# A fused retention and mixture-of-experts kernel on one core: the last shared-down tiles move behind the output product, and steps 7 to 9 are reordered

## What is computed

```
q, k, v, g = x@w + b            (8 heads of 32; q and k rotated)
sim   = (q k^T / sqrt(32)) * decay mask (causal)
ret   = group_norm(sim @ v) * gn_weight + gn_bias
x1    = layernorm(x + (silu(g) * ret) @ w_o + b_o)
shared = (silu(x1@shared_gate) * (x1@shared_up)) @ shared_down
routed = top-1 of 8 experts, score s = sigmoid(logit):
         (up * silu(gate)) @ down_proj, gate|up = (s*x1)@gate_up_proj
out   = layernorm(x1 + shared + routed)
```

## Time and profile before

| | us |
|---|---|
| median of three runs (lowest, highest) | 561.33 (559.33, 561.43) |
| the profiled execution, its own time | 561.59 |
| its span in the trace | 559.8 |
| TensorE busy | 538.6 (96%) |
| VectorE, ScalarE, GpSimd busy | 410.0, 229.4, 338.3 |
| SyncE | only starts transfers |
| mean granted clock of TensorE, share of full | 0.988 |

### The profile page before, as it was taken

How to read it: one execution, slowest core, us unless ns; L and a number is a source line. 1 busy time by engine, 2 the same in 40 slices (tenths; PEclk the granted TensorE clock), 3 DMA queues, 4 the chain that set the end, 5 groups by cost and what they waited for, 6 DMA issues and landing times.

```text
span 559.8 us, 11796 instructions
## 1 busy us (share of the span) xinstructions
PE 538.6 (96%) x3830; PEld 454.4 (81%) x3830; DVE 410.0 (73%) x892; ACT 229.4 (41%) x410; POOL 338.3 (60%) x330
## 2 busy tenths in 40 slices
PE   8999989999999999999997889999999999999994
PEld 6777778788788788788886678888888888888884
DVE  5896986887887887887974678757866666666664
ACT  4435532454553552552542765133333333333331
POOL 1956695475475575774683385716786556566644
PEclk9999999999999999999998899999999999999998
DMA  8920507605405306304296823765677666666651
GB/s 264 318 93 3 187 1 49 217 0 98 168 1 162 104 2 138 128 0 151 77 358 171 305 109 114 255 198 181 198 184 211 192 183 179 183 198 194 196 181 38
DMA packets 46554, 83.82 MB, mean 150 GB/s; under 512 B 11360, under 2 KB 30576, under 8 KB 46480
## 3 DMA queue, kind: packets, MB, share of 16 engines
q1 hardware_dynamic: 38720, 64.52, 37.4%
q0 software_dynamic: 6112, 15.40, 10.2%
q10 hardware_dynamic: 1664, 3.15, 1.6%
HBM read 61.11 MB, written 22.34 MB: 149 GB/s over the span
## 4 chain that ended last, share of the span: by engine, by line
PE 81%; POOL 5%; issue 5%; DVE 4%; DMA 4%; SPq 1%; ACT 1%; POOLq 0%; DVEq 0%; ACTq 0%
PE duo L1731 42%; PE duo L2190 9%; PE duo L2021 5%; PE duo L1811 4%; DMA dn_raw<-L_ffn_down_proj 4%; PE duo L1836 3%; PE duo L2200 3%; PE duo L1893 3%; PE duo L2025 2%; POOL rstd L1014 2%; PE duo L2011 1%; PE duo L2076 1%; PE duo L2003 1%; PE duo L1925 1%; POOL turned L977 1%
## 5 line engine op out<-in xcount | busy, mean ns | idle before, releaser
L1731 PE MATMUL duo<-w_gu_hi,xsT 128*128 x320 | 107.2, 397 | 0.0
L1731 PE MATMUL duo<-x1T,wsgu 128*128 128x512 f32 x384 | 91.1, 393 | 1.5 <-DVE x1T L1237 1.5
L1731 PEld LDWEIGHTS duo<-x1T,wsgu 128*128 128x128 f32 x384 | 71.4, 188 | 17.1 <-DVE x1T L1237 2.5
L1147 POOL DMA_INDIRECT out_rows<-of,seat x39 | 39.5, 1012 | 56.7 <-DVE of L1688 55.0
L1731 PEld LDWEIGHTS duo<-w_gu_hi,xsT 128*128 128x128 f32 x320 | 59.7, 188 | 11.2
L1731 PE MATMUL duo<-w_gu,xsT 128*128 x160 | 62.0, 388 | 0.0
L1643 DVE SCALAR_TENSOR_TENSOR eh<-duo,seat,e_act 128x512 f32<-128x512 f32 x38 | 28.5, 751 | 39.9 <-PE duo L1731 39.9
L1220 DVE TENSOR_TENSOR sims<-duo,causal 128x512 f32<-128x512 f32 x64 | 41.1, 684 | 21.0 <-ACT sims L719 20.4
L977 POOL TENSOR_TENSOR turned<-turned,swapped 128x1024 f32<-128x1024 f32 x16 | 38.5, 2405 | 29.7 <-DVE swapped L1211 29.7
L1138 POOL DMA_INDIRECT xz<-xz_d,seat x39 | 45.8, 1173 | 8.9 <-issue 8.8
L1077 POOL DMA_INDIRECT seat_d<-stage,place_i x32 | 35.7, 1117 | 18.9 <-DVE place_i L1479 9.6
(11 more groups left out here) (214 smaller groups left out, 1292.0 us busy)
## 6 DMA issues: line engine op xcount, KB each, us to landing
dn_rest<-dn_lo_d SPq DMA_DIRECT2D x39, 512.0 KB, 4.5
w_gu<-L_ffn_gate_up_proj SPq DMA_DIRECT2D x8, 1024.0 KB, 9.7
x_in<-x_t SPq DMA_DIRECT2D x8, 512.0 KB, 6.9
x_res<-L_attn_x SPq DMA_DIRECT2D x8, 512.0 KB, 4.0
dn_raw<-L_ffn_down_proj SPq DMA_DIRECT2D x8, 512.0 KB, 9.6
dn_hi_d<-dn_top SPq DMA_DIRECT2D x8, 512.0 KB, 7.5
dn_lo_d<-dn_low SPq DMA_DIRECT2D x8, 512.0 KB, 8.5
xz_d<-zs SPq DMA_DIRECT2D x8, 512.0 KB
```

The costliest lines, as they stand in the source:

```text
L1147: pool.indirect_dma_start(out, bass.IndirectOffsetOnAxis(ap=seat[:, s, 1:2], axis=0), of[:, s % OUTS, :], None).then_inc(sig.out_done[s % ...
L1731: last = mm(out_, left(a, k), right(b, k), start=start and k == 0 and n == 0, stop=stop and k == kt - 1 and n == len(PASSES) - 1)
```

## The change

Three things change.

1. **Deferral.** In steps 3 to 7 (`DEFERRED`) TensorE no longer takes `shared_down(f, 1)` ahead of `output(a)`. It takes it in the next step, between the second quad of `similarities` and the first of `values`. VectorE's `shared_sum(f, 1)` and SyncE's `sums_out` move with it into the next step (steps 4 to 8).
2. **Steps 7 to 9.** `PARTED` gives step 4 two experts (3 and 4) and step 7 one (7). In step 8 TensorE takes the second half of the last `gate_project`, behind `ret_transposes`; ScalarE, VectorE and the loads follow that (experts 1 and 3 change places, the load of expert 1 waits longer, the load of expert 0 starts earlier). `first_norm` of pair 6 is done in two parts, `statistics` and `moments` of it stand earlier on VectorE. The first product of step 9 takes its passes so that it needs the high half of `x1T` first.
3. **Group norm and step 2.** `group_rstd` works on each half as soon as its variance is there, in all steps. In step 2 `swap(2, 1)`, `turn(2, 1)`, `residual(1)` and `x_lo(3)` are taken later.

The core of the diff (line numbers are those of before):

```diff
 HALF_FF = FF // 2
-PARTED = {1: (0,), 2: (1,), 3: (2,), 4: (3,), 5: (4,), 6: (5,), 7: (6, 7)}
+PARTED = {1: (0,), 2: (1,), 3: (2,), 4: (3, 4), 5: (5,), 6: (6,), 7: (7,)}
+DEFERRED = range(3, PAIRS)
 SEATS = (EXPERTS - 1) * TOKENS + SLOTS * P
...
                     down_raw_in(PARTED[t][0])
+                if t - 1 in DEFERRED:
+                    sums_out(t - 3)
                 if has(t - 2):
...
                 if t == PAIRS - 1:
-                    sp.wait_ge(sig.g_ps, KT * PAIRS)
+                    sp.wait_ge(sig.qk_ps, 4 * PAIRS)
                     gate_up_in(0)
-                    gate_up_in(1)
                     sp.wait_ge(sig.turned_ok, 2 * PAIRS)
...
                 if t == PAIRS:
-                    sp.wait_ge(sig.o_ps, 2 * (PAIRS - 1))
-                    gate_up_in(7)
                     sp.wait_ge(sig.s_ps, 8 * PAIRS)
                     gate_up_in(2)
+                    sp.wait_ge(sig.o_ps, 2 * (PAIRS - 1))
+                    sp.wait_ge(sig.g_ps, KT * PAIRS)
+                    gate_up_in(1)
+                    gate_up_in(7)
                 if t == PAIRS + 1:
...
                     down_raw_in(PARTED[t][1])
-                if has(t - 2) and t < PAIRS:
+                if has(t - 2) and t < PAIRS and t not in DEFERRED:
                     sums_out(t - 2)
...
                     act.wait_ge(sig.g_ps, KT * PAIRS)
+                    act.wait_ge(sig.zs_ok, 2 * (PAIRS - 2))
                     act.wait_ge(sig.xT_lo, KT * PAIRS)
...
                             later_weights_hi()
+                        if t == PAIRS and j == 5:
+                            first_norm(f, [0])
                     ret_copy(a, 0)
...
                 if has(f):
-                    first_norm(f, [TILES - 1] if 2 < t < PAIRS else range(TILES))
+                    first_norm(f, [TILES - 1] if 2 < t < PAIRS else range(1, TILES) if t == PAIRS else range(TILES))
                     if t in PARTED and len(PARTED[t]) > 1:
...
                     if t == PAIRS:
+                        gate_act(a, [1])
                         expert_hi(0)
                 if has(t) and t > 1:
-                    gate_act(t)
+                    gate_act(t, [0] if t == PAIRS - 1 else range(KT))
                 if has(f):
                     if t == PAIRS:
-                        expert_hi(1)
+                        expert_hi(3)
                     if t == PAIRS + 1:
...
                     if t == PAIRS:
-                        expert_hi(3)
+                        expert_hi(1)
                     shared_act(f, 3)
...
             def group_rstd(a):
-                pool.wait_ge(sig.var_ok, 2 * a + 2)
-                nc.gpsimd.tensor_scalar(var_e[:, :], var[:, :], EPS, None, ALU.add).then_inc(sig.eps_ok, 1)
-                pool.wait_ge(sig.eps_ok, a + 1)
-                pool.wait_ge(sig.rn_ok, 2 * a)
                 for i in range(2):
                     half = slice(16 * i, 16 * i + 16)
+                    pool.wait_ge(sig.var_ok, 2 * a + i + 1)
+                    nc.gpsimd.tensor_scalar(var_e[:, half], var[:, half], EPS, None, ALU.add).then_inc(sig.eps_ok, 1)
+                    pool.wait_ge(sig.eps_ok, 2 * a + i + 1)
+                    pool.wait_ge(sig.rn_ok, at(2 * (a - 1) + i + 1))
                     nc.gpsimd.tensor_tensor(rstd[:, half], var_e[:, half], minus_half[:, half], ALU.pow)\
...
                         residual(a)
-                    turn(t, 1)
+                    if t != 2:
+                        turn(t, 1)
                     if t == 0:
...
                         group_rstd(a)
-                    if t < 3 or t == PAIRS:
+                    if t in (1, PAIRS):
                         residual(a)
...
                     take_seats(f)
+                if t == 2:
+                    residual(a)
+                    turn(t, 1)
                 if t in PARTED:
...
                     dve.wait_ge(sig.sq_ok, 2 * a + i + 1)
-                    dve.wait_ge(sig.eps_ok, a)
+                    dve.wait_ge(sig.eps_ok, at(2 * (a - 1) + i + 1))
                     nc.vector.tensor_reduce(var[:, 16 * i:16 * i + 16],
...
                 shared_product(f, 1)
-                expert_lo(3, 5)
+                expert_lo(1, 5)
                 for j in range(2, FT):
...
                 elif has(a):
+                    if t == PAIRS:
+                        statistics(f, [0, 1])
                     masked(a, 0)
                     if t == PAIRS:
-                        statistics(f, [0, 1])
+                        statistics(f, [2, 3])
+                        moments(f)
                     elif has(f):
...
                     masked(a, 1)
-                    if t == PAIRS:
-                        statistics(f, [2, 3])
-                        moments(f)
+                    if t - 1 in DEFERRED:
+                        shared_sum(f - 1, 1)
                     if has(t):
...
                         v_biased(t, [0])
-                    swap(t, 1)
+                    if t != 2:
+                        swap(t, 1)
                     if t > 2:
...
                     variance(a)
-                if has(t + 1) and t != 1:
+                if t == 2:
+                    swap(t, 1)
+                elif has(t + 1) and t != 1:
                     x_lo(t + 1)
...
                         choose(f)
+                        go_on(f)
                         group_norm(a, [1])
                         shared_product(f, 1)
-                        go_on(f)
                         find_seats(f)
...
                         dve.wait_ge(sig.nmr_ok, PAIRS)
-                        expert_lo(1, 3)
+                        expert_lo(3, 3)
                 if has(a) and t < PAIRS:
...
                     y_rest(a)
+                if t == 2:
+                    x_lo(t + 1)
+                if t == PAIRS:
+                    x1_lo(a)
                 if has(f):
                     shared_sum(f, 0)
-                    if t == PAIRS:
-                        x1_lo(a)
-                    if t <= PAIRS:
+                    if t not in DEFERRED and t <= PAIRS:
                         shared_sum(f, 1)
...
                     if a > 1:
-                        pe.wait_ge(sig.gate_ok, KT * (a + 1))
+                        pe.wait_ge(sig.gate_ok, KT * (a + 1) - (a == PAIRS - 1))
                         pe.wait_ge(sig.z_ok, 2 * (a - 1) + 1)
...
                     pe.wait_ge(sig.z_ok, 2)
+                if t == PAIRS - 1 and parts[0]:
+                    pe.wait_ge(sig.s_diag, 8 * PAIRS)
                 for n in parts:
...
                     if j == 0:
-                        pe.wait_ge(sig.x1T_lo, KT * (f + 1))
+                        pe.wait_ge(*((sig.x1T_hi, KT * (f + 1)) if f == PAIRS - 1 else (sig.x1T_lo, KT * (f + 1))))
                         if f == 0:
...
                             else:
-                                pe.wait_ge(sig.gate_ok, KT * (f + 3))
+                                pe.wait_ge(sig.gate_ok, KT * (f + 3) - (f + 3 == PAIRS))
                         elif has(f + 1):
                             pe.wait_ge(sig.s_diag, 8 * (f + 2))
+                            if j:
+                                pe.wait_ge(sig.gate_ok, KT * PAIRS)
                         else:
...
                         pe.wait_ge(sig.h_ok, FT * f + j - 1)
+                if f == PAIRS - 1 and i + j == 0:
+                    for n in (0, 2, 1):
+                        part, low = PASSES[n]
+                        if low:
+                            pe.wait_ge(sig.x1T_lo, KT * (f + 1))
+                        for k in range(KT):
+                            last = mm(duo[0][:, 0, :], wsgu[:, 0, part, k, 0:P], x1T[:, low, k, :],
+                                      start=n + k == 0, stop=low == 1 and k == KT - 1)
+                    last.then_inc(sig.gu_ps, 1)
+                    return
                 three(duo[j % 2][:, i, :], lambda part, k: wsgu[:, i, part, k, j * P:(j + 1) * P],
...
                             similarities(a, n)
+                            if t - 1 in DEFERRED and n == 1:
+                                shared_down(f - 1, 1)
                             if n:
...
                 if has(t) and t != 1:
-                    gate_project(t, [1] if t == 2 else range(KT))
+                    gate_project(t, [1] if t == 2 else [0] if t == PAIRS - 1 else range(KT))
+                if t == PAIRS:
+                    gate_project(a, [1])
                 if t == 1:
...
                         x1_transposes(a)
-                    shared_down(f, 1)
+                    if t not in DEFERRED:
+                        shared_down(f, 1)
                 if has(a) and t < PAIRS:
...
```

## The result

The changed kernel takes 561.55 us (median of 12 runs, 560.66 to 562.12). The kernel before, measured again beside it, takes 560.52 (12 runs, 559.33 to 561.43). The ratio is 1.0024, interval 1.0013 to 1.0035: the same within 0.5%. The forecast of 552.6 was wrong, and the time lies outside its range of 549.5 to 557. The profiled execution of after took 560.75 with a span of 558.9; it lies at the low end of its runs and that of before (561.59) at the high end of its own, so the traces differ by -0.9 us where the medians differ by +1.0.

What follows compares the result with a forecast made beforehand. TensorE, busy in 96% of the span, bounds the kernel; only its waits and slow clock can be gained. Step 8's start moves -4.5 - 1.8 + 0.5 - 0.5 = -6.3, start to output -2.4, together -8.7: 552.6 us, range 549.5 to 557.

Steps and rivals of the forecast that it cites:

- Step 2: Reorder on VectorE and GpSimd removes waits of 0.8 and 2.4 us and 1.7 of slow clock; net gain 4.5.
- The deduction: In step 2, x_lo(3) ahead of the output's sums may meet GpSimd's residual: 0.4 taken, at most 1.5 us.
- The deferral: Moving shared_down(f, 1) takes 1.8 us off step 3 into step 8, gains nothing between full steps.
- the boundaries: Output bound by y_rest in five steps, 0.1 us each: +0.5, bounds 0 to 2.
- Step 7: Half the gate product leaves, 1.4 us; only 0.5 gained, with a new wait of 0.9 for x1_lo.
- Step 8, start to G: From step 8's start to TensorE's gate-up (G): 14.3 us instead of 17.8, with 3.2 us more work.
- G to the output: Step 8, gate-up to output product: 14.0 us instead of 12.9, as ranked meets the residual add.
- rival 1: Step 8: choose gets through before GpSimd's residual add, 1.95 us less, 550.6; chance 0.25.
- Rival 2: Clock falls again in step 8 (1.7 us), or step 3 starts late (1.1 more): 554.3 to 555.4; chance 0.25.
- Rival 4: Most gain missing: deferral only moves step 8's wait, or expert 1's load is late; 557.3 to 559.9; chance 0.10.

Runs made afterwards that it cites:

- b2: Kernel before with only the reorder of step 2 (swap, turn, residual later), x_lo(3) staying early, group norm not halved; 555.86 us, ratio 0.9898.
- e1: Changed kernel with x_lo(3) back at its old place in the middle of step 2; 553.71 us, ratio 0.9888.
- e2: Changed kernel with GpSimd's down_rest of step 2 behind norm_scales of step 3, a run of two adds instead of three; 559.08 us, ratio 0.9978.
- e7: Changed kernel with x_lo(3) behind both sums of the shared down, in the middle of GpSimd's residual add; 560.81 us, ratio 0.9993.
- e3: e1 with the deferral from step 7 alone; 550.81 us, ratio 0.9832.
- e4: e1 with no deferral at all; 550.34 us, ratio 0.9824.
- e5: e4 with both halves of the last gate projection in step 7 again; 549.6 us, ratio 0.9787.
- e8: e4 with the variance's add in group_rstd taken whole again, the two powers still halves; 549.95 us, ratio 0.9792.
- e9: e5 with expert_lo(0) moved out of step 8 to between the first two shared products of step 9; 553.55 us, ratio 0.9851.
- e10: e5 with the variance's add whole and expert_lo(0) behind the product of y with the gate in step 8; 551.64 us, ratio 0.9857.
- b1: Kernel before with the new PARTED alone: experts 3 and 4 in step 4, 7 alone in step 7; 555.18 us, ratio 0.9894.
- e6: Changed kernel with x_lo(3) one operation later, behind the first sum of the shared down; 561.75 us, ratio 1.0006.

## Why the prediction was wrong

**Step 2, the step that failed.** The gain itself was well counted: 4.9 us before the deduction, 5.4 in b2. The deduction failed. The prediction let `x_lo(3)` meet GpSimd's residual and priced it at 0.4, at most "up to a whole add less the slack, 1.5 us". It measured 5.9 up to the start of step 3 and 1.2 of clock in it (e1 against the changed kernel). Two things were wrong in it. The distance was counted right, `x_lo` starts 0.9 us ahead of the residual, but `x_lo` is two instructions that start 0.6 apart, so that the second stood at 0.3 from the add; 0.4 was chosen as if the whole of it got through. And the bound took one add. The change itself put three of them in a row: it moved `residual` and `turn` behind the seat scatters, directly ahead of `down_rest`. The prediction had read `hT_lo` of the earlier trace rows, which came out between two adds (2.27 us), and took that for the rule; e2 and e7 show that here the whole run counts. The bound of 1.5 was missed by more than 4 us in the start of step 3 alone. What is behind the held instruction on VectorE, the sums that open step 3, had been named.

A rule of the Trainium skill bears on this (SBUF — State Buffer, "Who interferes with whom"): a VectorE instruction with two SBUF inputs and a GpSimd instruction that reads SBUF shut each other out for the whole instruction, and the one that issues first goes first. The first part agrees with the run of 2.4 us adds here and with GpSimd's 1.74 and 2.93 us rows beside `expert_lo(0)`. The second doesn't agree with the starts that the trace gives: `x_lo`'s second half started 0.3 us ahead of the residual and ended after it and two more. Nor does the power obey it as the holder: `expert_lo(0)` ran its usual 2.29 us from 319.58 though the first power lasted to 320.31.

**The deferral.** Out of step 3 it takes 1.4 us (41.53 in e3, 40.15 in e1), where -1.8 and +0.1 stood. That it fills 3.1 to 4.9 in step 8 "where TensorE would otherwise wait for `masked` of the second quad" was wrong: the first `values` need only `masked` of the first quad, which is there. e4 shows step 8 without them 1.7 us shorter. So the deferral moves work from a full step to a full step and gains nothing anywhere. At the boundaries the output did become bound by `y_rest`, as forecast, but at 0.6 us in each of steps 4 to 6 instead of 0.1. The 15 matmuls leave only 1.47 us where they stood (from `y_transposes` to the output 5.15 instead of 6.62), since the output now waits 0.17 to 0.33 for `yT_lo`; they cost 1.99 in their new place. The bound of 2 us for all five was too low; e1 against e3, which differ in four of them, gives 2.9 by the medians.

**Step 7** did not gain 0.5. It took 41.80 us; the wait for `x1_lo` is 0.72, near the 0.9 forecast, and the rest is the cost of the boundary again. By itself the gate half that moved away takes 0.37 off step 7 (41.19 in e4, 41.56 in e5), near the 0.5.

**Step 8, start to G:** 14.45 for the forecast 14.3, the waits at 0.46 and 0.83 where 0.9 stood. The sum came out although its reason for placing the deferred group there was wrong: without the group the stretch is 12.78 (e4), not 14.3. **G to the output:** 12.68 instead of 14.0, between the forecast and rival 1, by a cause that neither had. `ranked` came at G+6.8, as counted. The powers did not end at G+6.7 but at G+8.2, because of what the prediction left out: `expert_lo(0)` holds the second variance add for 1.4 us. So the residual add came too late to meet `choose`:

```profile
320.29 1.71 POOL L1018 TENSOR_SCALAR var_e<-var 128x16 f32<-128x16 f32 x1
322.08 2.93 POOL L1021 TENSOR_TENSOR rstd<-var_e,minus_half 128x16 f32<-128x16 f32 x1
324.98 2.37 POOL L1027 TENSOR_TENSOR x_res<-x_res,bias_o 128x1024 f32<-128x1024 f32 x1
```

```profile
319.58 2.29 DVE L1342 TENSOR_TENSOR w_gu<-w_gu,w_gu_hi 128x2048 fp32r<-128x2048 f32 x1 [2.05 <-ACT w_gu_hi L815]
...
324.09 0.19 DVE L1463 TENSOR_TENSOR hot<-ranked,first_of 128x32 fp32r<-128x32 f32 x1
...
325.05 0.69 DVE L1268 TENSOR_TENSOR y<-duo,rstd 128x512 f32<-128x512 f32 x1 [0.68 <-POOL rstd L1021]
```

Whether they would meet in the changed kernel's own arrangement without that hold was not tried. In e8, e9 and e10 the residual came 0.3, 0.3 and 0.5 us after the last product of `choose`; in e9 the norm is halved and nothing holds the add.

**Right:** both long waits had the causes named, and b1 and b2 take them away one by one (5.5 and 5.4 us of distance). Experts 3 and 4 in step 4 cost nothing, and behind the output of step 8 the distance changed by 0.3. Rival 2 had the right place, "step 3 starts late", but 1.1 us for it instead of 6, and with the slow clock there and not in step 8. Rival 4 had the right doubt about the deferral.

## What to carry over

When a change moves an operation in one engine's queue, count what the other engine has in a row there, after its own moves. In four kernels here a subtraction with both operands in SBUF was held for the whole run of adds, so bound such a meeting by the run, not by one instruction. In an engine that is full in every step, moving work to the next step gains only where a wait can be pointed to that ends later than the moved work; list for each wait the one operation that it needs. And take a large reorder apart: here one table entry and one reorder gave some 5.5 us each, and two other parts, the place of `x_lo(3)` and the deferral, took them back.

## What was not expected of the hardware

- A subtraction of VectorE with both operands in SBUF that started 0.3 us ahead of a GpSimd add of 2.4 us was held through three back-to-back adds, 7.9 us. In the kernel before a like one (`hT_lo`) came out between two adds, after 2.27 us, and the second add took 2.81 us instead of 2.4; b1 has the same pair (2.27 and 2.82). What decides between the two stays open; none of e2, e6 and e7 brought the second case.
- The hold goes the other way too: beside VectorE's `expert_lo` (2.29 us) an add of GpSimd over 128x16 took 1.7 us instead of 0.27, and a power over 128x4 took 2.93 instead of 1.04. A power of 2.93 us that had started already was not lengthened, and did not lengthen `expert_lo`; one that started inside `expert_lo` took 3.75 (e8).
- The clock fell to half after TensorE's waits of 2.16 (e9), 3.71, 4.0 and 5.97 us, and in steps 2 to 9 of these traces never after one of 1.2 or less. After a wait of 2.4 us it fell in the kernel before (0.62 over 4.5 us) and did not in b1, at the same place:

```profile
81.50:86.00 4.50, 4.50 (x40) 4.50 (x39) 3.77 (x7) 4.18 (x6) 3.30 (x3) 1.00 0.05 8
```

That profiled execution is also the fastest of b1's runs, which spread over 3.2 us, while those of b2, without the wait, spread over 0.4. The mean granted clock of each run fits this: three runs of b1 had 0.996 and took 553.9 to 554.5 us, the other three 0.992 or 0.993 and took 555.9 to 557.0. So the clock probably fell after the wait in half of them; where in the run it fell isn't recorded.
